# Four graph layers on 1 core: in the dense layers message and wide products alternate three quads apart, turned rows come a quad ahead, and ScalarE copies the column numbers and makes two of sixteen wide one-hots

## The reference, cut to what matters

```
x = layernorm(x + L0(x, src, dst, edge_weight))
x = layernorm(x + L1(x, src, dst))          # two GIN layers, below
x = layernorm(x + L2(x, edge_index, edge_attr))
x = layernorm(x + L3(x, edges))

def gin_layer(x, ...):
    agg = segment_sum(x[src], dst)          # 12500 x 128
    h = relu((x + agg) @ W1 + b1)           # 128 -> 32
    h = bn(h); h = h @ W2 + b2              # 32 -> 128
    return leaky_relu(bn(h))
```

## Time and profile before

| | |
|---|---|
| time, median of 3 runs | 13404.71 us (13402.66 to 13409.51) |
| the profiled execution's own time | 13400.2 us |
| its span | 13398.5 us |
| busy, share of the span | PE 58%, PEld 44%, DVE 74%, ACT 22%, POOL 51% |
| mean granted TensorE clock | 0.726 |
| dense stage, layer 0 and layer 1 | 4904 to 6664 us and 6778 to 8537 us |
| quads in it | 2 x 1128 |

### The profile page before, as it was taken

The page is one execution under the profiler, slowest core; times in us unless marked ns, Lnnn a source line. Parts: engine busy times, 40 slices in busy tenths (PEclk is TensorE's granted clock), DMA queues, the critical chain, the costliest instruction groups (busy, mean ns, idle before and its releaser), DMA issues.

```text
span 13398.5 us, 239237 instructions
## 1 busy us (share of the span) xinstructions
PE 7824.6 (58%) x49340; PEld 5915.0 (44%) x49341; DVE 9874.1 (74%) x39935; ACT 2937.9 (22%) x9903; POOL 6840.5 (51%) x7116
## 2 busy tenths in 40 slices
PE   5000000244444479999999999878888874444442
PEld 4000000243333355555555555478888863444442
DVE  8777777355444479999889999878888885556656
ACT  1000000000000043333333333356666650000000
POOL 2777777777777710000000000077777747777774
PEclk5555555555555579999989999999999995555555
DMA  4544445913111133333223333344445553333333
GB/s 122 168 148 147 147 150 163 73 56 52 52 52 52 52 85 84 84 84 84 74 66 84 84 84 84 96 129 130 131 131 131 130 139 79 80 80 80 80 80 86
DMA packets 1553047, 1311.69 MB, mean 98 GB/s; under 512 B 420058, under 2 KB 1415933, under 8 KB 1552285
## 3 DMA queue, kind: packets, MB, share of 16 engines
q1 hardware_dynamic: 1095700, 715.85, 21.7%
q0 software_dynamic: 224352, 469.74, 13.2%
q10 hardware_dynamic: 232626, 122.48, 3.4%
HBM read 1133.89 MB, written 173.47 MB: 98 GB/s over the span
## 4 chain that ended last, share of the span: by engine, by line
POOL 25%; DVE 21%; issue 12%; DVEq 3%; PE 2%; DMA 1%; ACT 0%; SPq 0%; POOLq 0%; ACTq 0%
POOL work L893 25%; DVE work L2023 14%; DVE work L2020 3%; DVE big L2033 2%; DVEq L2007 1%; DVEq L167 1%; DVE work L2016 0%; PE ps L1449 0%; DMA x_tab<-work 0%; DVE work L1966 0%; DVE work L1960 0%; PE ps L1469 0%; DVEq L2033 0%; PE ps L1436 0%; DVEq L2018 0%
## 5 line engine op out<-in xcount | busy, mean ns | idle before, releaser
L893 POOL DMA_INDIRECT work<-q_tab,pay_a x1760 | 1671.6, 950 | 2497.5 <-DVE big L1775 1961.7
L2023 DVE TENSOR_SCALAR work<-work 128x512 bf16<-128x512 f16 x9024 | 2558.2, 346 | 1.7 <-PE ps L1391 1.6
L1772 DVE TENSOR_TENSOR big<-big,ps 128x128 f32 (+1 forms) x5280 | 1494.5, 283 | 1319.7 <-PE ps L1266 917.9
L1391 PE MATMUL ps<-work 128*96 128x512 bf16 x9024 | 2392.6, 388 | 3.8
L893 POOL DMA_INDIRECT work<-h_tab,pay_a x1760 | 1671.0, 949 | 668.2 <-issue 535.8
L860 POOL DMA_INDIRECT edges_a<-work,big x1660 | 1695.1, 1021 | 551.5 <-issue 504.3
L893 POOL DMA_INDIRECT work<-in_x_dram,pay_a x1760 | 1692.1, 961 | 545.1 <-issue 535.9
L1266 PE MATMUL ps<-work 128*128 128x128 f32 x3520 | 902.3, 438 | 1487.7 <-DMA work<-in_x_dram,pay_a 843.0
L1042 ACT ACTIVATE work<-ps 128x384 bf16<-128x384 f32 x2256 | 1105.5, 490 | 2415.8 <-PE ps L1382 2415.8
L1541 PE MATMUL ps<-work 128*128 128x129 f32 x3520 | 917.0, 441 | 1218.1 <-DVE work L1764 1218.1
L1266 PEld LDWEIGHTS ps<-work 128*128 128x128 f32 x3520 | 779.1, 326 | 1599.8 <-issue 1503.0
(11 more groups left out here) (374 smaller groups left out, 13338.0 us busy)
## 6 DMA issues: line engine op xcount, KB each, us to landing
work<-pair_lo SPq DMA_DIRECT2D x2256, 128.0 KB
work<-edges_a SPq DMA_DIRECT2D x440, 256.0 KB
work<-lo_rows SPq DMA_DIRECT2D x880, 128.0 KB
pay_a<-key_rows SPq DMA_DIRECT2D x166, 640.0 KB
work<-in_edge_attr_dram ACTq DMA_DIRECT2D x166, 640.0 KB, 5.0
work<-in_x_dram,pay_a POOLq DMA_INDIRECT x1760
work<-q_tab,pay_a POOLq DMA_INDIRECT x1760
work<-h_tab,pay_a POOLq DMA_INDIRECT x1760
```

Of the source, the lines that this page charges most:

```text
L893: pool.indirect_dma_start(out=ring[:, at:at + width], out_offset=None, in_=table, in_offset=bass.IndirectOffsetOnAxis(ap=pay[:, e, 1:2], a ...
L1391: m = pe.matmul(ps[0:H3, 4 + kk // QUADS_G, :], lhsT=pair_msg[:, kk % 4, j * H3:(j + 1) * H3], rhs=pair_hot[:, kk % 4, j, :], start=kk % Q ...
L1772: dve.tensor_tensor(o, o, tile_sums, ALU.add).then_inc(p.acc, 1)
L2023: ins = dve.tensor_scalar(pair_hot[:, k % 4, j, :], iota_s[:, :], pair_at[:, k * 4 + j:k * 4 + j + 1], None, ALU.is_equal)
```

## The change

Nothing changes in what is computed: the same pairs, products and sums.

- TensorE: the wide products of quad `s - 3` (`LATE`) instead of `s - 2`, and one by one behind the message products of quad `s`: message 0, wide 0, message 1, wide 1 and so on. All waits stand ahead of the eight products. In the steady loop it no longer waits for `oh` (the wait for `oht` of `s` implies it, as VectorE makes the wide one-hots of `s - 2` before the turned one of `s`) nor for `staged` of `s - 4`. For quads 0 and 1 of each four it waits for ScalarE's one-hot (`hot`), which comes after the staging.
- VectorE: step `s` is now turned one-hot of `s`, then wide one-hots of `s - 1`, then the add of the group that began at `s - 8`; the span number is read first in the step. Two quads in four get three wide one-hots instead of four. The column copy is gone.
- ScalarE: after its message copy it makes the fourth one-hot of quads 0 and 1 of each four (`ACT_HOT = 2`) in two passes over 512 columns, `|column - number|` and then `relu(1 - that)`, the second behind a wait for the first; at the third quad of each four it copies the next sixteen column numbers.
- Two semaphores are made one, a `hot` is added, and a column of ones `pair_one` is set up.

```diff
             def message_out(l):
+                def columns(first, k):
+                    act.activation(pair_at[:, k * 4:k * 4 + 16], pair_dst[:, bass.ds(first * 4, 16)], ACT.Copy).then_inc(sums.pst, 1)
+
                 def step(s, k, u):
                     act.wait_ge(sums.smm, s + (l * QUADS + 1))
                     wait(act, sums.mm, s + (GROUPS + l * QUADS - 3))
                     act.activation(pair_msg[:, k % 4, :], ps[:, k % 4, 0:4 * H3], ACT.Copy).then_inc(sums.staged, 1)
+                    if k % 4 == 2:
+                        wait(act, sums.oh, s + (GROUPS + l * QUADS - 2))
+                        columns(s + 2, (k + 2) % RING)
+                    if k % 4 < ACT_HOT:
+                        hot = pair_hot[:, k % 4, 3, :]
+                        done = hots_of_act(l, k, u)
+                        if k % 4 == 0:
+                            act.wait_ge(sums.pst, columns_in(l, k, u))
+                        act.activation(hot, iota_s[:, :], ACT.Abs, scale=-1.0, bias=pair_at[:, k * 4 + 3:k * 4 + 4]).then_inc(sums.hot, 1)
+                        act.wait_ge(sums.hot, done - 1)
+                        act.activation(hot, hot, ACT.Relu, scale=-1.0, bias=pair_one).then_inc(sums.hot, 1)
...
             def pair_sums(l):            # TensorE
                 def step(s, k, u):
+                    g, (kk, gu) = s - LATE, back(k, u, LATE, RING)
                     if live(s, QUADS):
                         bl = load_blocks(ONLY_PE, blk_row, s)
                         pe.wait_ge(sums.oht, s + (l * QUADS + 1))
-                        wait(pe, sums.staged, s + (l * QUADS - 3))
-                        for j in range(4):
-                            m = pe.matmul(... message product j of quad s ...)
-                        m.then_inc(sums.smm, 1)
-                    g, (kk, gu) = s - 2, back(k, u, 2, RING)
                     if live(g, QUADS):
-                        pe.wait_ge(sums.staged, g + (l * QUADS + 1))
-                        pe.wait_ge(sums.oh, g + (GROUPS + l * QUADS + 1))
+                        if not live(s, QUADS):
+                            pe.wait_ge(sums.oh, g + (GROUPS + l * QUADS + 1))
+                        if kk % 4 < ACT_HOT:
+                            pe.wait_ge(sums.hot, hots_of_act(l, kk, gu))
+                        else:
+                            pe.wait_ge(sums.staged, g + (l * QUADS + 1))
                         if kk % QUADS_G == 0:
                             wait(pe, sums.acc, gu * 2 + (kk // QUADS_G + TILES + l * PAIR_GROUPS - 1))
-                        for j in range(4):
-                            m = pe.matmul(... wide product j of quad g ...)
-                        m.then_inc(sums.mm, 1)
-                run_steps(pe, QUADS, RING, 2, step)
+                    for j in range(4):
+                        if live(s, QUADS):
+                            m = pe.matmul(... message product j of quad s ...)
+                        if live(g, QUADS):
+                            m = pe.matmul(... wide product j of quad g ...)
+                run_steps(pe, QUADS, RING, LATE, step)
...
             def pair_sums(l):            # VectorE
                 def step(s, k, u):
+                    q, (kq, uq) = s - 1, back(k, u, 1, RING)
+                    g, (kg, ug) = s - 8, back(k, u, 8, RING)
+                    flush = kg % QUADS_G == 0 and live(g, QUADS)
+                    if flush:
+                        group = ug * 2 + kg // QUADS_G
+                        v = load_span(group)
                     if live(s, QUADS):
-                        if k % 4 == 0:
-                            dve.tensor_copy(pair_at[:, k * 4:k * 4 + 16], pair_dst[:, bass.ds(s * 4, 16)]).then_inc(sums.pst, 1)
-                            dve.wait_ge(sums.pst, u * 2 + (GROUPS + l * (QUADS // 4) + k // 4 + 1))
...
-                        wait(dve, sums.mm, s + (GROUPS + l * QUADS - 3))
-                        for j in range(4):
-                            ins = dve.tensor_scalar(pair_hot[:, k % 4, j, :], ...)
+                    if live(q, QUADS):
+                        if kq % 4 == 0:
+                            dve.wait_ge(sums.pst, columns_in(l, kq, uq))
+                        wait(dve, sums.mm, q + (GROUPS + l * QUADS - 3))
+                        for j in range(3 if kq % 4 < ACT_HOT else 4):
+                            ins = dve.tensor_scalar(pair_hot[:, kq % 4, j, :], ...)
```

More of the change, by code:

```diff
@@ L63, in __init__ @@
     def __init__(self, sem):
-        self.turned, self.kept, self.cells, self.sums = sem("pair_turned"), sem("pair_kept"), sem("pair_cells"), sem("pair_sums")
+        self.turned, self.kept, self.cells = sem("pair_turned"), sem("pair_kept"), sem("pair_cells")
         self.cmp, self.mm, self.list = sem("pair_cmp"), sem("pair_mm"), sem("pair_list")
@@ L493, in gnn_program @@
         ident_h = take((P,), BF16)
+        pair_one = take((1,))
         take = carver(work, 0)
@@ L568, in gnn_program @@
         LIST_AT, CMP_AT = 50, 74
+        ACT_HOT, LATE = 2, 3
         BATCHES = QB // 4
@@ L1042, in step @@
                     act.activation(pair_msg[:, k % 4, :], ps[:, k % 4, 0:4 * H3], ACT.Copy).then_inc(sums.staged, 1)
+                    if k % 4 == 2:
[9 more added lines that the diff above has]
+                        act.activation(hot, hot, ACT.Relu, scale=-1.0, bias=pair_one).then_inc(sums.hot, 1)
+                act.wait_ge(pairs.cells, 5)
+                act.wait_ge(sums.pst, GROUPS + l * (QUADS // 4 + 1))
+                act.wait_ge(sums.oh, GROUPS + l * QUADS)
+                columns(0, 0)
                 run_steps(act, QUADS, RING, 0, step)
@@ L1303, in _ @@
                     pe.matmul(ps[:, 4, 0:SPANS], lhsT=before_f[:, :], rhs=cell_t[2], start=True, stop=True)
-                    pe.matmul(ps[:, 5, 0:SPANS], lhsT=ones[:, :], rhs=cell_t[2], start=True, stop=True).then_inc(pairs.sums, 1)
+                    pe.matmul(ps[:, 5, 0:SPANS], lhsT=ones[:, :], rhs=cell_t[2], start=True, stop=True).then_inc(pairs.turned, 1)
                 if s == LIST_AT + 18:
@@ L1307, in _ @@
                     pe.matmul(ps[:, 7, 0:SPANS], lhsT=shift_f, rhs=offs_p[:, 1:SPANS + 1], start=True, stop=False)
-                    pe.matmul(ps[:, 7, 0:SPANS], lhsT=wrap_f, rhs=offs_p[:, 0:SPANS], start=False, stop=True).then_inc(pairs.sums, 1)
+                    pe.matmul(ps[:, 7, 0:SPANS], lhsT=wrap_f, rhs=offs_p[:, 0:SPANS], start=False, stop=True).then_inc(pairs.turned, 1)
             pe.wait_ge(pairs.cells, 4)
@@ L1828, in pair_starts @@
             def pair_starts():
-                dve.wait_ge(pairs.sums, 1)
+                dve.wait_ge(pairs.turned, 3)
                 ch(dve.tensor_scalar(turn_i, ps[:, 5, 0:SPANS], float(QG - 1), None, ALU.add))
@@ L1842, in pair_steps @@
             def pair_steps():
-                dve.wait_ge(pairs.sums, 2)
+                dve.wait_ge(pairs.turned, 4)
                 ch(dve.tensor_tensor(step_f, offs_p[:, 1:SPANS + 1], ps[:, 7, 0:SPANS], ALU.subtract))
@@ L1995, in _ @@
             ch.sync()
-            dve.memset(pair_at, 0.0).then_inc(pairs.cells, 1)
+            dve.memset(pair_one, 1.0).then_inc(pairs.cells, 1)
             dve.wait_ge(pairs.cells, 5)
@@ L2020, in step @@
                         dve.tensor_scalar(pair_turn[:, k % 4, :], pair_bc[:, k % 4, :], iota_p[:, 0:1], None, ALU.is_equal).then_inc(sums.oht, 1)
[L2021 to L2029 removed]
+                    if live(q, QUADS):
[3 more added lines that the diff above has]
+                        for j in range(3 if kq % 4 < ACT_HOT else 4):
+                            ins = dve.tensor_scalar(pair_hot[:, kq % 4, j, :], iota_s[:, :], pair_at[:, kq * 4 + j:kq * 4 + j + 1], None, ALU.is_equal)
+                        ins.then_inc(sums.oh, 1)
+                    if flush:
                         dve.wait_ge(sums.mm, g + (GROUPS + l * QUADS + QUADS_G))
@@ L2032, in step @@
                         at = acc_t[0:H3, bass.ds(v * SPAN, SPAN)]
-                        dve.tensor_tensor(at, at, ps[0:H3, 4 + half, :], ALU.add).then_inc(sums.acc, 1)
-                run_steps(dve, QUADS, RING, 7, step)
+                        dve.tensor_tensor(at, at, ps[0:H3, 4 + kg // QUADS_G, :], ALU.add).then_inc(sums.acc, 1)
+                run_steps(dve, QUADS, RING, 8, step)
                 dve.wait_ge(sums.acc, TILES + (l + 1) * PAIR_GROUPS)
```

12 lines of the change are left out of this document (10 added, 2 removed).

## The result

The changed kernel takes 12902.3 us (median of 4 runs, 12900.5 to 12904.9) against 13403.7 (4 runs, 13401.8 to 13409.5) for the kernel before in the same comparison: ratio 0.9624, 95% interval 0.9609 to 0.964. It is 501 us faster where 458 were forecast; 12947 was predicted, within the range of 12885 to 13180.

What follows compares the result with a forecast made beforehand. TensorE's issue (1.355 us a quad) was taken to bound the changed kernel, just over VectorE (1.33): (1.560 - 1.356) x 2256 = 460 us saved, 13400.2 - 460 + 2 = 12942, as a median 12947; range 12885 to 13180.

Steps and rivals of the forecast that it cites:

- VectorE's term, 1.33 a quad: Dense layers: VectorE's work without column copy and two of sixteen wide one-hots, 5.33 us per four quads, 1.33 a quad.
- TensorE's term, 1.355: Dense layers: TensorE's instruction issue after dropping two of four waits in a step, 1.355 us a quad, bounds 1.30 to 1.45.
- The 1.42: TensorE's own step in the kernel before when catching up: mean 1.42 us a quad over six steps without the loop branch.
- VectorE stays the bound: Rival for the dense layers: TensorE's issue is under 1.33 us a quad, time 12893; chance 0.15.
- Removing VectorE work alone would stop at about 1.45: Dense layers: with only VectorE relieved, TensorE's own pace would hold the period at about 1.45 us a quad.
- the gap from the last message load to the first wide load: TensorE's step: this gap, 0.16 us on average, disappears with the dropped waits; some 0.04 stays.
- The array: TensorE's array under the issue: a message and wide pair takes 0.26 to 0.29 us, four 1.03 to 1.15, under 1.355.
- alternation gives the array nothing: Rival on TensorE: no weight load runs beside a product, 1.52 to 1.56 us a quad, time 13310 to 13405; chance 0.05.
- The issue can't run ahead: Rival on TensorE: issue stays within about one product of the array, step 1.73 us, time 13790; chance 0.06.
- ScalarE: Dense layers: passes of 0.71 us; ScalarE needs about 4.7 of 5.42 us per four quads, no added table loads.
- The ring of message, ScalarE and wide product: Loop of TensorE and ScalarE: 5.05 of 5.42 us per four quads, 0.37 spare; rival that ScalarE's chain decides, 13159, chance 0.16.
- SP and the ends: SP's turned-key loads stay hidden with 2.5 us to spare; the fuller pipeline costs 1 us at each layer's end.

Runs made afterwards that it cites:

- e2: Kernel before, VectorE making two wide one-hots a quad, each read twice, TensorE's order and waits untouched: 1.457 and 1.480 us a quad in layers 0 and 1.
- e1: Changed kernel, VectorE making two wide one-hots a quad, each read twice, ScalarE none: 1.326 and 1.337 us a quad in layers 0 and 1.
- e9: Changed kernel, with TensorE reading the block numbers of two quads in one load instead of one load a quad: 12893.8 us.
- e11: Changed kernel, with one block-number load for two quads and ScalarE making five wide one-hots in eight quads instead of four: 12820.4 us.
- e4: Changed kernel with TensorE's old step (four waits, old order), three quads apart as in the change: 1.468 and 1.492 us a quad, 178 us gained.
- e3: Changed kernel with the same waits, but four message products and then four wide ones: 1.334 and 1.344 us a quad in layers 0 and 1.
- e7: Changed kernel with wide products two quads behind the message products instead of three: 1.605 and 1.606 us a quad, 111 us slower than the kernel before.
- e6: Changed kernel with ScalarE making three of sixteen wide one-hots instead of two: 1.427 us a quad in both layers.
- e12: Changed kernel once more, unaltered, as yardstick on the chip of e9 and e11: 12905.5 us.
- e8: Changed kernel with VectorE making all sixteen wide one-hots and copying the column numbers, ScalarE only copying messages: 15399.6 us against 15458.0 for the kernel before.

## Why the prediction was right, and where it was off

**VectorE's term, 1.33 a quad: right.** 1.330 by its starts, full in layer 0. In layer 1 its wide one-hots stand still once a lap for some 0.07 us, for a buffer that TensorE frees: behind one turned one-hot of a lap the first wide one starts after 0.327 us there and after 0.265 in layer 0. The busy share of 99.9% doesn't show this, as the recorded durations overlap.

**TensorE's term, 1.355: too large by 0.018 to 0.029.** This is the step that failed in size. It consisted of 1.42 - 0.12 + 0.05 + 0.01. The 1.42 holds: the seven steps without the branch have a mean of 1.42 in layer 0 of e2. The same seven have 1.28 in e1, so 0.13 went and not 0.12; the branch adds 0.33 to 0.35 in one step of eight, 0.04 and not 0.05; the alternation adds nothing. That gives 1.33 for layer 0; layer 1 is 0.011 slower, for a register operation that the last section shows; the forecast, made from steps of layer 0, left it out. The forecast took the larger of 1.33 and 1.355 where both are 1.33, and (1.356 - 1.335) x 2256 = 47 us are the miss of 45. The rival "VectorE stays the bound" (12893) misses by 9 us and is nearer in time than the forecast; it is true of layer 0. The forecast's own picture, TensorE's issue as the larger term, is true of layer 1 alone and there by 0.007. The prediction had the two 0.025 apart. As both came out near 1.33, the time hardly says which of them decides; e1 and e9 to e11 say it.

**"Removing VectorE work alone would stop at about 1.45": right in kind.** e4 stops at 1.48, e2 at 1.468. That the waits have to go as well is the heart of the forecast, and e4 with e3 shows it. The forecast priced what went as the gap from the last message load to the first wide load, less 0.04, in all 0.12. By the starts in e2 and e1 it is 1.13 register operations a quad at 0.11 each, 0.13: the right place, and a little more of it.

**The array: right in size, beside the point.** Pairs are 0.26 apart, the lower end of 0.26 to 0.29. 96 and 512 columns at the 0.216 of 512 would be 608 / 512 x 0.216 = 0.257, so both weight loads are hidden. The Trainium skill, "TensorE: Matmul & The Clock Gate", section "Part 3: Packing small matmuls — row/col tiling", lets a load overlap a running product only where the row groups differ; here all loads and products use the same rows, and the spacing disagrees with it. The same section also speaks of a load that goes to a background weight buffer and is pulled ahead, which the prediction passed over and with which the spacing agrees; no run here shows where a load goes. The rival "alternation gives the array nothing" fails on the same rows, though in another sense it was true: e3 shows that there was nothing for it to give.

**"The issue can't run ahead": refuted.** After the fourth pair starts at 5402.32, the next message load stands at 5402.74, 0.42 later. The 0.33 us load of block numbers starts at 5402.0 in the trace, before that pair, so it runs beside the pairs. The prediction gave the rest of a step 0.74; where it can't run ahead, all of that would lie behind the last pair.

**ScalarE: right.** A pass was taken at 0.71; it takes 0.71 and 0.72. Its need was put at 4.7 of 5.42 per four quads; it is 4.35 of 5.33 (82% by the table), since the second pass follows the first within 0.03 us and not 0.1. The kernel has four table loads of 1.28 us, as before, and none in the dense stage. The Trainium skill, "ScalarE: Activation LUTs", section "Table sets: the hidden batching unit", says that abs and relu are in every set, and the trace agrees. The ring of message, ScalarE and wide product was put 0.37 away from deciding; e7, with a quad less of distance, is past that point, and e6 shows the other way in which ScalarE can decide.

**SP and the ends: right.** The turned keys never make VectorE wait; the pipeline's ends cost about 1 us.

## What to carry to other kernels

When two engines look full, measure each one's own pace before choosing an edit: take half of the work off one, leave all of the other's instructions in place, and read the period; an edit to one of two engines that tie looks worthless alone (12 or 4 us here) and is worth more together with its partner (85 here). On TensorE's queue a wait costs issue time even when it is long fulfilled, above all by the register operations that work out its value: a wait that another one implies is worth deleting, while reordering the products around it brought next to nothing.

## What the runs showed of the hardware

In TensorE's sequencer a register operation of a wait costs about 0.11 us of issue and not the 0.032 of its row (e1 and e2, e3 and e4). Semaphore instructions, 0.051 by their row, start 0.106 ahead of the next instruction; these kernels have nearly as many of them before as after, so what a deleted one gives back wasn't measured.

The recorded duration of a VectorE instruction is not what it costs. In layer 0 of the changed kernel the one-hots are recorded at 0.66 in the fence above and at a mean of 515 ns over the kernel, growing from 0.41 in the first 200 us of layer 0 to 0.77 near its end; in layer 1, the same instruction at the same spacing is short again:

```profile
7001.57 0.34 DVE L2057 TENSOR_SCALAR work<-work,iota_p 128x512 bf16<-128x512 bf16 x1
7001.84 0.87 DVE L2063 TENSOR_SCALAR work<-work 128x512 bf16<-128x512 f16 x3
7002.62 0.34 DVE L2057 TENSOR_SCALAR work<-work,iota_p 128x512 bf16<-128x512 bf16 x1
```

In e12, the same kernel again, the mean is 338 ns, at nearly the same 10.65 and 10.72 us a lap. Why the record grew in one execution isn't settled; start-to-start it is 0.2625 in all of them.

A wait of an engine for its own last instruction is cheap on ScalarE (0.03 us between the passes) and dear on VectorE (0.21 to 0.23 in the earlier trace rows). On VectorE copy and wait cost 0.39 behind the add (before) and 0.29 behind the turned one-hot (e8); which neighbour makes the difference wasn't tested.

Layer 1 issues 0.011 us a quad slower than layer 0 from the same lines of the kernel. One instruction of the step has another duration there, the register operation ahead of the block-number load; the rows are from 5000 to 6300 and from 6600 to 7900 us of the changed kernel:

```profile
L647 PEldq FUSED_REGOPS  x854: 55/55/55, 5001.6 to 6297.8; - x171
```

```profile
L647 PEldq FUSED_REGOPS  x849: 69/69/69, 6601.2 to 7898.9; - x170
```

In e1 the load starts 0.114 after it in layer 0 and 0.128 in layer 1, in seven steps of eight, which makes 0.012 a quad: the whole difference. Why it is longer was not tested.
